# Two attention layers: the product with the values two steps behind the scores instead of one

## The chip, the cores and the metric

The kernel runs on one core of a Trainium2 chip, in one launch. The metric is the device time of that launch in microseconds, the median of the runs; lower is better.

## The reference, cut to what matters

Four layers on x of 4 sequences x 1024 tokens x 128 channels. Each layer normalises x, computes s (a mixer) and g (a network), and sets `x = x + s * silu(g)`. The mixers are a state-space layer, two causal softmax attentions with 16 heads of 8 channels, and a linear attention; the networks are a quantized one, one with low-rank parts, and two with experts. The change concerns the two softmax attentions alone:

```python
# layer 1
scores = jnp.einsum('bhqd,bhkd->bhqk', q, k) / math.sqrt(dh)
scores = scores + alibi_bias(H, L, scores.dtype)[None]      # causal, -inf above the diagonal
attn = jax.nn.softmax(scores, axis=-1)
out = jnp.einsum('bhqk,bhkd->bhqd', attn, v)
...
# layer 2: q and k turned by rope, then
scores = jnp.einsum('bhqd,bhkd->bhqk', q, k) * D ** (-0.5)
scores = jnp.where(causal[None, None], scores, -jnp.inf)
weights = jax.nn.softmax(scores, axis=-1)
out = jnp.einsum('bhqk,bhkd->bhqd', weights, v)
```

## The kernel before, in words

`attention_layer` is called once for layer 1 and once for layer 2. Its work is cut into 16 groups (`NGB`), each of 4 heads of one sequence. A group has two chunks of 512 queries (`ch`), and runs over 12 steps (`key_steps`): blocks of 128 keys (`j`), 4 for the first chunk, 8 for the second. Because of causality the steps differ in width: the queries that see the block are 512, 384, 256 and 128 in steps 0 to 3; 512 in steps 4 to 8; 384, 256 and 128 in steps 9 to 11.

A step has two `scores` events, one for each pair of heads: PE multiplies keys by queries into one of two PSUM buffers (`sring`, tile a_st, L1530), with a mask product on the diagonal (L1533); ACT takes the exponential into `prob`, which has three buffers, one per step (L1653). Then a `values` event: four products of 9 columns (8 channels and the row sum) with the probabilities, one per head, go into the accumulator `acc`, each head into 32 partitions of its own (L1548). Since scores lie with keys on partitions, the row maximum has to be known before: for every group, one group ahead, `max` events compute queries by keys (tile a_mx, L1497, mask L1500 or L1492), DVE reduces each (L1743); when a chunk is complete DVE does six small operations on the maxima (L1749 to L1754), PE transposes them (`turn_max`, L1506), DVE copies, and SP sends them through DRAM into three extra rows of the queries.

When the last step of a chunk is accumulated, ACT copies `acc` into `osb` (L1660); the next chunk's first `values` waits for that copy. A `turn_out` event transposes `osb` on PE (L1558), and DVE divides by the row sums (L1764, L1770).

The results of `max`, `turn_max`, `turn_out` and of the projections share one ring of three PSUM buffers (`qring`, tile a_mx) in the order of the program: an event waits until the event three places before it has been emptied, by DVE or for some kinds by ACT.

All engines walk through the same list `order`, each doing its part, and wait for each other by counting semaphores. The list is made by a loop over groups, steps and pairs: at each score index (24 per group) it puts the events of other work that are due (projections of the next sequence, in layer 2 the scatters by POOL), then as many `max` events as a table of due times says, then `scores`. `values` of step s-1 comes after the scores of step s; the last step's comes at the end of the group. The turned output of the second chunk is put before the scores of step 2 of the next group, that of the first chunk after step 6. The main waits on PE:

```python
                            if s >= 2:
                                pe.wait_ge(exped, s - 1)       # scores number s of the layer
...
                            pe.wait_ge(exped, 2 * (v + 1))     # values number v of the layer
...
                            if j == 0 and chunk:
                                pe.wait_ge(o_evac, chunk)
```

Of the kernel before, what the change touches and what calls it, by code (L numbers as in the profile page):

```python
# [98 lines left out]
def build_program(nc, a, out, ctx):  # L99
# [1032 lines left out]
    def attention_layer(layer, seqs, loads, x_slots=None):  # L1132
# [10 lines left out]
        NGB = NG * BATCH  # L1143
        QB4 = NT // 2
        MROWS = PARTS * GH * QB4
        NP_, NR = 3, 3
        STEPS = 24


# [20 lines left out]
        for G in range(1, NGB):  # L1170
            due[STEPS * G + 8 - LEAD] = unit_end[2 * G + 1]
        due[STEPS * NGB] = len(ahead)
        due_at, due_n = sorted(due), [due[k] for k in sorted(due)]
        key_steps = [(ch, j) for ch in range(2) for j in range(4 * ch + 4)]
# [55 lines left out]
        placed_at.sort(key=lambda v: v[0])  # L1230

        order, done, put = list(prelude), 0, 0
        late = None
        for G in range(NGB):
            for s, (ch, j) in enumerate(key_steps):
                for pair in range(2):
                    index = STEPS * G + 2 * s + pair
                    while put < len(placed_at) and placed_at[put][0] <= index:
                        order.append(placed_at[put][1])
                        put += 1  # L1240
                    goal = math.ceil(np.interp(index, due_at, due_n))
                    order += ahead[done:goal]
                    done = max(done, goal)
                    if (s, pair) == (2, 0) and G:
                        order.append(("turn_out", G - 1, 1))
                    order.append(("scores", G, ch, j, pair))
                if s:
                    order.append(("values", G, *key_steps[s - 1]))
                if s == 6:
                    order.append(("turn_out", G, 0))  # L1250
            order.append(("values", G, *key_steps[-1]))
        order.append(("turn_out", NGB - 1, 1))
        order += [e for _, e in placed_at[put:]] + back_events(BATCH - 1)

        at = {}
# [20 lines left out]
        with ExitStack() as c:  # L1276
# [30 lines left out]
            else:  # L1307
# [10 lines left out]
            ring_made, ring_v, ring_a, m_ready, st_made, exped, pv_done, o_evac, step, astep = (  # L1318
                sem(n + k) for k in ("ring_made", "ring_v", "ring_a", "m_ready", "st_made", "exped", "pv_done", "o_evac",
                                     "step", "astep"))  # L1320
# [1540 lines left out]
```

## Time and profile before

| | |
|---|---|
| median of 3 runs | 2873.87 us |
| lowest, highest | 2872.76, 2879.74 us |
| span of the profiled execution | 2867.6 us, 6.3 us under the median of the runs; its own time outside the profiler is not known |
| PE | 2232.3 us busy (78%) |
| DVE | 1650.8 us busy (58%) |
| ACT | 1246.7 us busy (43%) |
| POOL | 727.9 us busy (25%) |

All times in the views are microseconds from the start of the span. PE is the matmul engine and PEld its weight loads, which run ahead of the matmuls; DVE, ACT and POOL are the vector, scalar and GpSimd engines, SP the queue that issues most DMAs. In a timeline row stand the start, the duration, the engine, the line, what is written from what, shapes and types, and the number of instructions merged in the row; in brackets the idle time of the engine before it and what ended it. The ends of matmuls are modelled and overlap the next start, so that on PE the distance between two starts is the cost of the first. A `values` event shows as 8 matmuls.

### The profile page before, as it was taken

To read this page: it belongs to the slowest core of one execution; us is meant where nothing else is said; L and a number is where in the kernel's file an instruction comes from. 1 tells how busy PE (TensorE), PEld (TensorE's weight loads), DVE (VectorE), ACT (ScalarE), POOL (GpSimd) and SP (SyncE) were. 2 spreads that over 40 slices of the span, in tenths; PEclk is the share of its full clock that TensorE was granted. 3 is DMA by queue.
4 is the path that set the end of the run, shared out by engine and by line. 5 is a ranking of instruction groups with operands and counts; after the bars stand their busy time and mean duration, and the time that the engine had idled before them with its cause. 6 is when DMAs were issued, how large, how long until landed. Compare 5 with 4: busy or idle time off the path is not lost. (4 is left out here: it accounts for less than half of the span.)

```text
span 2867.6 us, 44223 instructions
## 1 busy us (share of the span) xinstructions
PE 2232.3 (78%) x15437; PEld 1302.5 (45%) x15454; DVE 1650.8 (58%) x3303; ACT 1246.7 (43%) x1901; POOL 727.9 (25%) x870
## 2 busy tenths in 40 slices
PE   3778878863899989999740389999999788777474
PEld 2555555542344444444340134444443686455274
DVE  6676767631677747567049277777775343553201
ACT  2343434320466656565520046565666343332143
POOL 1435353441010101000000223233322113663432
PEclk8898888876899999999755599999999899896597
DMA  2111100012011101110000302121210895110185
GB/s 62 39 53 53 46 2 2 2 44 85 2 55 40 54 24 32 46 36 20 1 1 3 106 22 77 42 79 40 79 54 27 257 321 185 41 41 22 38 274 182
DMA packets 144303, 185.77 MB, mean 65 GB/s; under 512 B 26970, under 2 KB 118267, under 8 KB 138976
## 3 DMA queue, kind: packets, MB, share of 16 engines
q1 hardware_dynamic: 103295, 137.52, 16.0%
q0 software_dynamic: 13696, 32.02, 3.5%
q10 hardware_dynamic: 27126, 13.75, 1.7%
q8 instruction: 117, 1.92, 0.3%
q14 instruction: 69, 0.57, 0.1%
HBM read 130.46 MB, written 52.21 MB: 64 GB/s over the span
## 5 line engine op out<-in xcount | busy, mean ns | idle before, releaser
L1743 DVE TENSOR_REDUCE a_mpart<-a_mx 128x1 f32<-128x512 f32 (+3 forms) x1216 | 741.2, 655 | 284.4 <-PE a_mx L1497 148.8
L1653 ACT ACTIVATE a_prob<-a_st 128x1024 f32<-128x1024 f32 (+3 forms) x768 | 607.1, 812 | 487.8 <-PE a_st L1533 374.4
L1497 PE MATMUL a_mx<-a_ka,a_qa 96*128 96x512 bf16 (+3 forms) x1536 | 428.8, 339 | 31.6 <-DVE a_mpart L1743 14.4
L1530 PE MATMUL a_st<-a_qa,a_ka 96*128 96x512 bf16 (+3 forms) x1536 | 416.3, 333 | 29.9 <-ACT a_prob L1653 22.8
L1548 PE MATMUL a_acc<-a_prob,a_v_aug 128*9 128x512 f32 (+3 forms) x3072 | 321.1, 494 | 0.0
L1497 PEld LDWEIGHTS a_mx<-a_ka,a_qa 96*128 96x128 bf16 x1536 | 140.7, 99 | 315.6 <-DVE a_mpart L1743 175.4
L1426 POOL DMA_INDIRECT x_rows<-l_xn,l_slots x128 | 125.4, 980 | 400.0 <-ACT a_prob L1653 390.0
L1533 PE MATMUL a_st<-w_mask_t,identb 128*128 128x128 bf16 x1024 | 208.8, 224 | 0.0
L1530 PEld LDWEIGHTS a_st<-a_qa,a_ka 96*128 96x128 bf16 x1536 | 145.7, 99 | 136.5 <-ACT a_prob L1653 38.6
L2084 PE MATMUL t_psu<-t_xsT,t_w 128*128 128x128 f32 x960 | 152.8, 294 | 23.9 <-DMA t_w<-in_l_experts 17.4
L1500 PE MATMUL a_mx<-w_mask_q,identb 128*128 128x128 bf16 x768 | 165.2, 225 | 0.0
L1968 POOL DMA_INDIRECT b_back<-y_rows,l_slots x128 | 134.1, 1048 | 71.8 <-issue 36.3
L2084 PEld LDWEIGHTS t_psu<-t_xsT,t_w 128*128 128x128 f32 x960 | 130.1, 203 | 36.6 <-issue 25.4
L1079 POOL TENSOR_TENSOR l_sqr<-l_yg 128x256 f32<-128x256 f32 x64 | 39.3, 614 | 280.2 <-DVE l_yg L932 277.6
L1533 PEld LDWEIGHTS a_st<-w_mask_t,identb 128*128 128x128 bf16 x1024 | 102.2, 100 | 15.5 <-issue 2.6
L2201 DVE TENSOR_TENSOR t_h<-t_sg,t_psu 128x128 f32<-128x128 f32 x160 | 45.9, 288 | 101.9 <-ACT t_sg L2149 98.6
L903 DVE TENSOR_TENSOR_SCAN l_lmat<-l_job,l_ident 128x1024 f32<-128x1024 f32 x32 | 73.1, 2288 | 45.2 <-PE l_job L564 44.7
L1548 PEld LDWEIGHTS a_acc<-a_prob,a_v_aug 128*9 128x9 f32 x3072 | 45.9, 88 | 109.8 <-issue 81.1
L1465 POOL TENSOR_TENSOR x<-x,a_prod 128x512 f32<-128x512 f32 x8 | 10.2, 1269 | 309.4 <-DVE a_prod L1831 309.4
L1764 DVE RECIPROCAL a_rden<-a_mx 128x16 f32<-128x16 f32 x64 | 16.1, 252 | 122.4 <-PE a_mx L1558 122.4
L1500 PEld LDWEIGHTS a_mx<-w_mask_q,identb 128*128 128x128 bf16 x768 | 77.1, 100 | 13.5 <-issue 8.3
L1436 POOL TENSOR_TENSOR l_xn<-x,a_st 128x512 f32<-128x512 f32 x8 | 8.1, 1040 | 281.9 <-DVE a_st L1777 281.9
(438 smaller groups left out, 4055.0 us busy)
## 6 DMA issues: line engine op xcount, KB each, us to landing
t_w<-in_l_experts SPq DMA_DIRECT2D x160, 192.0 KB, 4.2
t_w<-in_l_experts SPq DMA_DIRECT2D x40, 514.0 KB, 7.4
a_qa<-q_parts_dram SPq DMA_DIRECT2D x96, 192.0 KB
a_ka<-k_parts_dram SPq DMA_DIRECT2D x96, 192.0 KB
x_rows<-zeros SPq DMA_DIRECT2D x25, 512.0 KB, 3.6
t_xs<-x_rows ACTq DMA_DIRECT2D x40, 256.0 KB, 4.9
y_rows<-t_y POOLq DMA_DIRECT2D x40, 256.0 KB, 5.1
q_parts_dram<-a_parts SPq DMA_DIRECT2D x24, 256.0 KB, 3.0
```

What stands on the lines that cost most here:

```text
L903: dve.tensor_tensor_scan(to, flat(e), ident8[:].rearrange("p t i -> p (t i)"), 0.0, ALU.mult, ALU.add).then_inc(ring_v, 1)
L1426: pool.indirect_dma_start(x2_rows, bass.IndirectOffsetOnAxis(x_slots[:, k, b * NT + t:b * NT + t + 1], 0), seqs[b].xn[:, t], None, bounds_ ...
L1497: ins = pe.matmul(to, qa[G % NQ][:, h0 + k, qi * P:(qi + 1) * P], ka[G % NQ][:, h0 + k, lo:hi], start=not masked_first, stop=k == per - 1 ...
L1500: ins = pe.matmul(to[:, width - P:width], identb[:], diagonal, start=False, stop=True)
L1530: ins = pe.matmul(to[:, lo:HALF], ka[G % NQ][:, h, j * P:(j + 1) * P], qa[G % NQ][:, h, ch * HALF + lo:(ch + 1) * HALF], start=True, stop= ...
L1533: ins = pe.matmul(to[:, lo:lo + P], identb[:], W["mask_t"][:], start=False, stop=True)
L1548: ins = pe.matmul(acc[h * SLOT:h * SLOT + DH + 1, lo:HALF], v_aug[:, b % 2, j, G % NG * GH + h], prob[:, v % NP_, h, lo:HALF], start=j == ...
L1653: act.activation(prob[:, v % NP_, 2 * pair:2 * pair + 2, lo:HALF], sring[s % 2][:, :, lo:HALF], ACT.Exp, scale=1.0 if alibi else scale).th ...
L1743: dve.tensor_reduce(mpart[:, G % 2, h0:h0 + per, qi, piece], slot[:, 0:per * width].rearrange("p (k w) -> p k w", k=per), X, ALU.max).then ...
L1968: pool.indirect_dma_start(dst, None, rows, bass.IndirectOffsetOnAxis(slots[:, t:t + 1], 0), bounds_check=rows.shape[0] - 1).then_inc(arriv ...
L2084: ins = pe.matmul(psu[k % 4][:, m * P:(m + 1) * P], w[:, k, m * P:(m + 1) * P], rhs, start=True, stop=True)
L2201: dve.tensor_tensor(h[:, k % 4], sg[:, k % 4], psu[k % 4][:, P:2 * P], ALU.mult).then_inc(h_ready, 1)
```

## The change

The loop now keeps a list `steps` of all `values` events of the layer, and puts the one that lies two steps back (`BACK = 2`) after each step's scores, across the ends of groups too; only the last two of the layer stand together, at its end. The turned output of the second chunk moves from before step 2 to before step 4 of the next group, that of the first chunk from after step 6 to after step 7. Nothing else changes: the same instructions, buffers and waits.

```diff
         NP_, NR = 3, 3
+        BACK = 2
         STEPS = 24
...
         order, done, put = list(prelude), 0, 0
-        late = None
+        steps = [("values", G, *step) for G in range(NGB) for step in key_steps]
...
-                    if (s, pair) == (2, 0) and G:
+                    if (s, pair) == (4, 0) and G:
                         order.append(("turn_out", G - 1, 1))
                     order.append(("scores", G, ch, j, pair))
-                if s:
-                    order.append(("values", G, *key_steps[s - 1]))
-                if s == 6:
+                current = len(key_steps) * G + s
+                if current >= BACK:
+                    order.append(steps[current - BACK])
+                if s == 7:
                     order.append(("turn_out", G, 0))
-            order.append(("values", G, *key_steps[-1]))
-        order.append(("turn_out", NGB - 1, 1))
+        order += steps[len(steps) - BACK:] + [("turn_out", NGB - 1, 1)]
```

All lines behind the first edit have numbers higher by one in the changed kernel.

Two places show what moves. The first is on PE, in layer 2, at the end of one group (number 6 of 0 to 15). Before, from the last scores of the group (keys and queries in buffers ka0, qa0) to the first of the next (ka1, qa1); the maxima (mx) are of the group after:

```order
4983 L1530 MATMUL a2_st1<-a2_qa0,a2_ka0 128x128
4984 L1533 MATMUL a2_st1<-w_mask_t,identb 128x128
4985 L1548 MATMUL a2_acc<-a2_prob,a2_v_aug 9x256 x4
4986 L1548 MATMUL a2_acc<-a2_prob,a2_v_aug 9x128 x4
4987 L1497 MATMUL a2_mx0<-a2_ka2,a2_qa2 128x384
4988 L1500 MATMUL a2_mx0<-w_mask_q,identb 128x128
4989 L1497 MATMUL a2_mx1<-a2_ka2,a2_qa2 128x384
4990 L1500 MATMUL a2_mx1<-w_mask_q,identb 128x128
4991 L1530 MATMUL a2_st0<-a2_qa1,a2_ka1 128x512
```

The changed kernel at the same scores, and its next block behind the two scores of the new group's step 0:

```order
4982 L1531 MATMUL a2_st1<-a2_qa0,a2_ka0 128x128
4983 L1534 MATMUL a2_st1<-w_mask_t,identb 128x128
4984 L1549 MATMUL a2_acc<-a2_prob,a2_v_aug 9x384 x4
4985 L1498 MATMUL a2_mx0<-a2_ka2,a2_qa2 128x384
...
4997 L1531 MATMUL a2_st1<-a2_qa1,a2_ka1 128x512
4998 L1534 MATMUL a2_st1<-w_mask_t,identb 128x128
4999 L1549 MATMUL a2_acc<-a2_prob,a2_v_aug 9x256 x4
5000 L1498 MATMUL a2_mx0<-a2_ka2,a2_qa2 128x512
```

The blocks of steps 10 (9x256) and 11 (9x128) stood together; now step 9's (9x384) ends the group, and step 10's follows the new group's first scores.

The second place is on PE, some rows further, at steps 1 and 2 of the new group. Before:

```order
5014 L1530 MATMUL a2_st1<-a2_qa1,a2_ka1 128x384
5015 L1533 MATMUL a2_st1<-w_mask_t,identb 128x128
5016 L1548 MATMUL a2_acc<-a2_prob,a2_v_aug 9x512 x4
5017 L1497 MATMUL a2_mx1<-a2_ka2,a2_qa2 128x512
5018 L1558 MATMUL a2_mx2<-ident,a2_osb 128x128 x4
...
5023 L1497 MATMUL a2_mx0<-a2_ka2,a2_qa2 128x512
5024 L1506 MATMUL a2_mx1<-identb,a2_mparts 48x128
```

The changed kernel there, and down to its turned output before step 4:

```order
5015 L1549 MATMUL a2_acc<-a2_prob,a2_v_aug 9x128 x4
5016 L1498 MATMUL a2_mx1<-a2_ka2,a2_qa2 128x512
...
5021 L1498 MATMUL a2_mx2<-a2_ka2,a2_qa2 128x512
5022 L1507 MATMUL a2_mx0<-identb,a2_mparts 48x128
...
5040 L1549 MATMUL a2_acc<-a2_prob,a2_v_aug 9x384 x4
5041 L1498 MATMUL a2_mx1<-a2_ka2,a2_qa2 128x512
5042 L1498 MATMUL a2_mx2<-a2_ka2,a2_qa2 128x512
5043 L1559 MATMUL a2_mx0<-ident,a2_osb 128x128 x4
```

Between the last score of step 1 and the transposed maxima (48x128) a block of 128 columns stands where one of 512 stood, and the turned output (from osb) is gone from there.

## Rows read from the trace of the kernel before

**Rows 1.** Windows: layer 1, layer 2, a group, the last group; per engine busy (x).
```profile
750.60:1432.00 681.40, 628.35 (x4658) 297.03 (x4656) 430.63 (x907) 411.34 (x536) 47.63 (x42) 0.95 0.11 33
1652.40:2222.30 569.90, 549.53 (x4283) 243.42 (x4284) 423.30 (x887) 339.59 (x458) 167.02 (x163) 0.99 0.18 53
1919.58:1952.29 32.71, 32.03 (x263) 14.00 (x262) 26.11 (x57) 19.87 (x27) 5.84 (x6) 1.00 0.18 52
2197.66:2222.30 24.64, 22.15 (x192) 7.81 (x185) 1.10 (x4) 19.62 (x27) 4.86 (x5) 1.00 0.05 15
```

**Rows 2.** Waits in layer 2: who waited for whom, us, times, longest.
```profile
PEld a_mx L1497 <- DVE a_mpart L1743: 91.9, 161, 1.3
```

**Rows 3.** The accumulator's tile, whole span: what its instructions waited for, us, times.
```profile
  ACT a_prob L1653: 22.2, 60
  PE a_acc L1548: 17.7, 32
```

**Rows 4.** Timeline of PE's weight loads at a group's end.
```profile
1918.24 0.12 PEld L1548 LDWEIGHTS a_acc<-a_prob,a_v_aug 128*9 128x9 f32 x8
1918.78 0.12 PEld L1548 LDWEIGHTS a_acc<-a_prob,a_v_aug 128*9 128x9 f32 x8 [0.42 <-ACT a_prob L1653]
1919.12 0.10 PEld L1497 LDWEIGHTS a_mx<-a_ka,a_qa 96*128 96x128 bf16 x1 [0.22 <-issue]
```

**Rows 5.** Timeline of PE: blocks of the values with their neighbours.
```profile
1895.97 0.62 PE L1548 MATMUL a_acc<-a_prob,a_v_aug 128*9 128x256 f32 x8
1896.52 0.39 PE L1497 MATMUL a_mx<-a_ka,a_qa 96*128 96x512 bf16 x1
...
1922.99 1.05 PE L1548 MATMUL a_acc<-a_prob,a_v_aug 128*9 128x512 f32 x8
1923.97 0.39 PE L1497 MATMUL a_mx<-a_ka,a_qa 96*128 96x512 bf16 x1
...
1926.14 0.22 PE L1533 MATMUL a_st<-w_mask_t,identb 128*128 128x128 bf16 x1
1926.20 0.27 PE L1530 MATMUL a_st<-a_qa,a_ka 96*128 96x256 bf16 x1
...
1926.32 0.22 PE L1533 MATMUL a_st<-w_mask_t,identb 128*128 128x128 bf16 x1
1926.46 0.83 PE L1548 MATMUL a_acc<-a_prob,a_v_aug 128*9 128x384 f32 x8
1927.23 0.39 PE L1497 MATMUL a_mx<-a_ka,a_qa 96*128 96x512 bf16 x1
```

**Rows 6.** Timeline of PE at steps 1 and 2 of a group.
```profile
1924.20 0.60 PE L1558 MATMUL a_mx<-ident,a_osb 128*128 128x128 f32 x4
1924.64 0.27 PE L1530 MATMUL a_st<-a_qa,a_ka 96*128 96x256 bf16 x1
...
1925.26 0.39 PE L1497 MATMUL a_mx<-a_ka,a_qa 96*128 96x512 bf16 x1
1925.86 0.24 PE L1506 MATMUL a_mx<-identb,a_mparts 128*48 128x128 bf16 x1 [0.20 <-DVE a_mpart L1743]
```

**Rows 7.** Timeline of DVE, the same stretch.
```profile
1919.56 3.77 DVE L1743 TENSOR_REDUCE a_mpart<-a_mx 128x1 f32<-128x384 f32 x6 [0.87 <-PE a_mx L1500]
...
1924.52 1.28 DVE L1743 TENSOR_REDUCE a_mpart<-a_mx 128x1 f32<-128x512 f32 x2
```

**Rows 8.** Timeline of PE behind the first chunk's turned output.
```profile
1904.23 0.66 PE L1558 MATMUL a_mx<-ident,a_osb 128*128 128x128 f32 x4
1904.72 0.33 PE L1497 MATMUL a_mx<-a_ka,a_qa 96*128 96x384 bf16 x1
...
1905.76 0.22 PE L1500 MATMUL a_mx<-w_mask_q,identb 128*128 128x128 bf16 x1
1906.03 0.39 PE L1497 MATMUL a_mx<-a_ka,a_qa 96*128 96x512 bf16 x1
```

**Rows 9.** Timeline of ACT: the accumulator's copies at the last group's start and end.
```profile
2197.91 0.59 ACT L1660 COPY a_osb<-a_acc 128x512 f32<-128x512 f32 x1 [0.53 <-PE a_acc L1548]
2221.57 0.59 ACT L1660 COPY a_osb<-a_acc 128x512 f32<-128x512 f32 x1 [0.53 <-PE a_acc L1548]
```

**Rows 10.** Timeline of PE at step 11 of a group.
```profile
1917.68 0.34 PE L1497 MATMUL a_mx<-a_ka,a_qa 96*128 96x384 bf16 x1 [0.20 <-DVE a_mpart L1743]
```

## The prediction

> **What bounds the kernel now.** First the busy time by stretch [rows 1]: the two attention layers take 681.4 and 569.9 us, nearly half of the span of 2867.6 us, and the change touches nothing else. In the second, PE is busy 549.5 of 569.9 us, DVE 423.3 and ACT 339.6: PE sets the pace. A group (four heads of one sequence) that carries no projections takes 32.71 us, and PE is busy for 32.03 of them. So what counts is what PE's own queue loses. Next the waits [rows 2]: PE's weight loads for the row maxima wait for DVE 161 times, 91.9 us in all; a load may wait early while PE still multiplies, so this is a bound, and the true loss must be read from PE's timeline. Last the values tile [rows 3]: its loads waited for the exponential 22.2 us in 60 cases, and ACT waited 17.7 us in 32 cases (one per group) for the last product of a group before it could copy the accumulator out. These two waits are what the change aims at.
>
> **Are they real?** Inside a group no values product waits for anything. Scores number n wait until exponential n-2 is done; scores (s, pair 1) thus wait for the last exponential of step s-1, and the product of step s-1 follows behind. Its wait is met when PE gets there, at a distance of one as of two. The exception is the group's end, where the products of steps 10 and 11 stand in a row. There [rows 4] the product of step 10 begins at 1918.24, that of step 11 at 1918.78, the next maximum at 1919.12. Step 10's product has 256 columns, and one that stands alone takes 1896.52 - 1895.97 = 0.55 us [rows 5]: as long as the 0.54 here. The load's wait of 0.42 us lies wholly under it. The change can win nothing on PE at the group's end.
>
> **Costs of the blocks.** A product of 512 columns takes 0.98 us, one of 384 0.77 (1926.46 to 1927.23) [rows 5], 256 0.55, 128 0.34 (1918.78 to 1919.12) [rows 4]. Before each block PE loses some time: 1926.32 to 1926.46 is 0.14 us for a mask product of 128 columns that otherwise takes 0.06 (1926.14 to 1926.20) [rows 5]. So 0.08 to 0.09 go at each entry, and blocks with it cost 1.07, 0.86, 0.64 and 0.43. A pair in a row pays one entry; the change splits it in 30 of 32 groups (the last of each layer stays a pair): 30 x 0.08 = 2.4 us. Does leaving the block cost too? The Trainium skill, TensorEngine Tiling (Array Packing), section Tiling Modes, says that changing the tiling mode drains TensorE; the products use 32 columns of the array each, their neighbours all of it. If that held on the way out as well, the 0.12 us by which 0.98 exceeds 4 x 512 columns at 2.4 GHz would belong to the switch, and the term would be 6 us. The trace speaks against it: in the pair, step 10's product shows the same 0.54 with no switch behind it. I take 2.4.
>
> **The moved work against DVE's ring.** Maxima, the transposed maxima and the turned outputs share three buffers that DVE empties, so PE waits where it issues them faster than DVE works. I follow the group from 1919.12, writing the shift of the changed kernel against the trace.
> (1) Before the last two maxima of the group stands step 9's block (0.86) instead of the pair (0.98): -0.12.
> (2) DVE reduces six blocks from 1919.56 to 1923.33, and its next reduction starts at 1924.52 [rows 7], since six small operations for the chunk's maxima lie between (1.19 us). Step 10's block (0.64) now stands in the midst of the six: DVE, fed about 0.4 us late, starts these small operations 0.47 later. PE waits here in both kernels. Before, the maximum at 1925.26 and the transposed maxima at 1925.86 wait for DVE's reductions [rows 6]: PE could have been there 0.29 and then 0.37 us sooner, 0.66 together. Now the turned output is gone from between, and the transposed maxima need the buffer one reduction (0.6) earlier: 1925.86 + 0.47 - 0.6 = 1925.73, shift -0.13. But by then PE has done less: the 1.07 block and the turned output (0.44, 1924.20 to 1924.64) are still to come, for 0.64 + 0.43. The wait has grown from 0.66 to about 1.1.
> (3) In step 2 follows 1.07 instead of 0.86: +0.08.
> (4) Steps 3 to 5 have blocks 0.86, 0.64, 0.43 instead of 0.64, 0.43, 1.07: -0.21; the turned output is paid here, +0.44, and the second maximum behind it waits for a buffer, about +0.22 (DVE needs some 1.8 us, with start and two reductions of 0.6 to 0.7, for what PE issues in 1.6). Shift +0.53.
> (5) The other turned output goes from step 6 to step 7. Behind it PE waited: 1905.76 to 1906.03 is 0.27 for 0.06, plus 0.05 in the 0.49 us from 1904.23 [rows 8]. In step 7 it stands after full blocks with DVE idle: -0.25. Shift +0.28.
> (6) In step 10 the block is 1.07 instead of 0.86. PE waits for DVE behind it (0.20 shown as idle before the maximum at 1917.68 [rows 10], some 0.7 in all three waits there), which swallows the 0.21.
> So such a group loses about 0.28 us, the extra entry of 0.08 included. Groups with projections have PE work of another kind between: there the wait in (4) goes, and the waits of (2) are partly DVE's for the projections. Followed the same way: +0.14 for one of the four kinds, +0.3 and +0.06 for the others. Mean 0.2, times 30 is 6 us; ends 0 and 0.5 (no wait added in (2) and (4), or both everywhere), 0 to 15 us.
>
> **The last group and the first.** The last has no maxima beside it; 24.64 us [rows 1], ACT and PE take turns. ACT's first copy waits 0.53 us there [rows 9], which the change removes, but the blocks move one step towards the end, where exponentials are short and PE sets the pace: one more 1.07 block behind the full ones, less what ACT and PE catch up. I get the last copy (2221.57 [rows 9]) 0.7 us later, 1.4 for two layers; ends -1 and +2.1. The first groups lack one block before they are under way: -0.6, ends 0 and -1.
>
> Other queues: SP's loads and POOL's scatters wait for exponentials counted by scores, whose order stays. The third buffer of exponentials is free before it is needed, since product s-3 stands in PE's queue before scores s. Cost nothing; if PE ran late there, scores would be late too.
>
> **Sum**: 6 + 1.4 - 0.6 = 6.8 us on 2867.6, a span of 2874.4. The median shown is 6.3 us above that span, so 2880.7.
>
> **Rivals.** (A) ACT's wait and copy at the group's end do count: 0.53 + 0.59 us for 30 groups would be 34 us, 2840. Against it: ACT is busy 60% of the time. A weaker form is likelier: the spread turned outputs save the waits of (2) and (5), 0.66 + 0.25, and nothing takes their place; less the 0.08 that is 0.83 x 30 = 25 us, 2849. For it: a 0.5 us DVE job leaves the tightest spot. Against it: six small operations stay, and PE's cover goes as well. Together 9%.
> (B) The wait behind the transposed maxima: it grows from 0.66 to 1.1 in all groups and the one of (4) comes everywhere, so 0.5 us per group, 15 us, 2889. It decides once a group loses over 0.29 us on average, since 0.3% (about what a measurement of this kernel can tell from no change) is 8.6 us. My own sum is near that point. 38%.
> (C) The distance is of no consequence at all: waits just change places. Then 2.4 us, 2876; it shares the verdict of my forecast. Forecast and (C) 53%.
>
> **Numbers.** Likeliest 2880.7, within 0.3%. Range 2864 to 2892: above it (B) with 1 us more per layer, below a gain of 10 us. Faster 9%, same 53%, slower 38%.
>
> **What would show it.** ACT's wait for the accumulator gone from all but the last groups: right by construction. The pair split, with blocks of 0.55 and 0.34 us and an entry before each. The group at 1919.58, 32.71 us long, at 33.0. PE's idle time before the transposed maxima up by some 0.4 us a group, behind the turned output of step 6 gone. If that group comes out at 32.3 or less, step (2) is wrong and a rival of gain holds; at 33.3 or more, (B).

## The result, and the profile after

| | before | changed |
|---|---|---|
| median of 20 runs each | 2876.51 us | 2886.48 us |
| lowest, highest | 2861.44, 2892.02 us | 2876.79, 2896.15 us |
| ratio | | 1.0039, 95% interval 1.0024 to 1.0053 |
| span of the profiled execution | 2867.6 us | 2884.2 us (its own time 2886.17) |

The change makes the kernel slower by 0.39%, some 10 us. The forecast was no measurable change, with 6.8 us lost. The measured time lies inside the range, but by the bound of 0.3% it is the slower case that came true; the interval still holds that bound. The profiled execution of before was a short one: its span lies 8.9 us below the median of the 20 runs, where a kernel's own time exceeds its span by 2.0 us (2886.17 against 2884.2). So the difference of the two spans, 16.6 us, is more than the change costs by about the 6.9 us by which that execution was short.

The windows of the changed kernel that answer to [rows 1], layer 1, layer 2, the group without projections and the last group (window, length, then busy us and count of PE, PEld, DVE, ACT and POOL, granted clock, share of the DMA engines, GB/s):

```profile
754.10:1443.00 688.90, 631.64 (x4654) 298.10 (x4653) 430.65 (x905) 408.63 (x536) 47.47 (x42) 0.94 0.12 32
1663.20:2241.00 577.80, 552.68 (x4283) 246.03 (x4283) 421.20 (x887) 336.02 (x458) 166.96 (x163) 0.98 0.18 52
1935.41:1968.44 33.03, 31.77 (x263) 14.05 (x262) 26.02 (x57) 19.65 (x26) 5.83 (x6) 1.00 0.19 51
2216.10:2241.00 24.90, 23.10 (x204) 8.15 (x200) 1.10 (x4) 19.04 (x27) 4.85 (x5) 1.00 0.05 15
```

The group went from 32.71 to 33.03 us, as forecast (33.0), and PE is busy 0.26 us less in it: what was added is waiting. ACT, DVE and POOL do the same work as before. But both layers grew by more than the groups explain, and the granted clock fell by 0.01 in each. The windows of [rows 1] and these do not end at the same event. Taken from the first scores to the start of the accumulator's last copy (before at 2221.57, [rows 9], changed in the row below), the last group of layer 2 went from 23.8 us (2197.78 to 2221.57) to 24.6 (2216.10 to 2240.68), layer 1 grew by 8.8 us (679.0 to 687.8) and layer 2 by 8.3 (569.2 to 577.5).

```profile
2240.68 0.58 ACT L1661 COPY a_osb<-a_acc 128x512 f32<-128x512 f32 x1 [1.02 <-PE a_acc L1549]
```

The tile of the accumulator (what its instructions waited for, us, times), beside [rows 3]:

```profile
  ACT a_prob L1654: 15.8, 43
  PE a_acc L1549: 3.0, 2
```

ACT waited for the accumulator 32 times and now does twice, at the end of each layer. What the change aims at has happened. The first row still has 43 cases at a distance of two steps: a weight load goes early and waits while PE still multiplies, so most of this row never was PE's time.

PE's timeline of the group without projections, from its first values block down to step 4, beside [rows 6]:

```profile
1936.89 0.62 PE L1549 MATMUL a_acc<-a_prob,a_v_aug 128*9 128x256 f32 x8
1937.44 0.39 PE L1498 MATMUL a_mx<-a_ka,a_qa 96*128 96x512 bf16 x1
...
1939.48 0.41 PE L1549 MATMUL a_acc<-a_prob,a_v_aug 128*9 128x128 f32 x8
1939.82 0.39 PE L1498 MATMUL a_mx<-a_ka,a_qa 96*128 96x512 bf16 x1
...
1940.38 0.38 PE L1498 MATMUL a_mx<-a_ka,a_qa 96*128 96x512 bf16 x1
1941.74 0.24 PE L1507 MATMUL a_mx<-identb,a_mparts 128*48 128x128 bf16 x1 [0.98 <-DVE a_mpart L1744]
...
1942.35 1.04 PE L1549 MATMUL a_acc<-a_prob,a_v_aug 128*9 128x512 f32 x8
1943.33 0.39 PE L1498 MATMUL a_mx<-a_ka,a_qa 96*128 96x512 bf16 x1
...
1945.98 0.60 PE L1559 MATMUL a_mx<-ident,a_osb 128*128 128x128 f32 x4
```

The pair is split, into blocks of 0.55 (1936.89 to 1937.44) and 0.34 us (1939.48 to 1939.82). A maximum of 512 columns takes 0.23 us from its start to the next start (1937.44 to 1937.67 on this timeline); the one at 1940.38 is followed by the transposed maxima only at 1941.74. So PE waits 1.36 - 0.23 = 1.13 us here, where before it waited 0.66 in two pieces. The 1.07 us block now stands behind the wait and not before it. The same place on DVE's timeline:

```profile
1937.92 1.89 DVE L1744 TENSOR_REDUCE a_mpart<-a_mx 128x1 f32<-128x512 f32 x3 [0.79 <-PE a_mx L1501]
...
1940.91 0.17 DVE L1755 TENSOR_TENSOR a_mparts<-a_mneg,a_mparts 128x16 bf16<-128x16 f32 x1
1941.01 1.88 DVE L1744 TENSOR_REDUCE a_mpart<-a_mx 128x1 f32<-128x512 f32 x3
```

DVE ends the last of its six small operations at 1941.08, goes on with a reduction, and when that has freed its buffer (0.6 us after 1941.01), PE's transposed maxima may start. From 1937.92 on it does not idle until the maxima are out: the ring of three buffers bounds PE here, as step (2) had it. Before that it stood idle for 0.79 us, since PE had step 10's block to do first; the six reductions that stood together in [rows 7] are now three and three, and the small operations start later.

Then the part that no step of the forecast spoke of. Windows of 2 us in group 1 of layer 2, same columns:

```profile
1722.00:1724.00 2.00, 0.68 (x6) 0.31 (x4) 1.81 (x7) 1.79 (x4) 0.72 (x1) 1.00 0.00 0
1724.00:1726.00 2.00, 1.75 (x13) 0.50 (x13) 1.51 (x4) 0.60 (x1) 1.88 (x2) 0.66 0.11 37
1726.00:1728.00 2.00, 2.00 (x14) 0.62 (x7) 0.52 (x1) 0.00 (x0) 0.28 (x1) 0.50 0.04 6
1728.00:1730.00 2.00, 2.00 (x22) 1.00 (x21) 1.46 (x3) 1.27 (x3) 0.31 (x1) 0.99 0.38 51
```

PE was busy for only 0.68 us of the first window. This kind of group (1, 5 and 9 of the layer) has 20 us of POOL's work beside it, and here the wait before the transposed maxima is the longest of the groups 1 to 14. Shortly afterwards the granted clock is at 0.50, the level of 1.2 GHz, and back at 2.4 GHz just after 1728. PE's timeline there and at the same place of group 5:

```profile
1724.25 0.24 PE L1507 MATMUL a_mx<-identb,a_mparts 128*48 128x128 bf16 x1 [1.57 <-DVE a_mpart L1744]
...
1725.00 1.90 PE L1549 MATMUL a_acc<-a_prob,a_v_aug 128*9 128x512 f32 x8
1726.83 0.61 PE L1498 MATMUL a_mx<-a_ka,a_qa 96*128 96x512 bf16 x1
...
1871.74 0.24 PE L1507 MATMUL a_mx<-identb,a_mparts 128*48 128x128 bf16 x1 [1.57 <-DVE a_mpart L1744]
...
1872.35 1.04 PE L1549 MATMUL a_acc<-a_prob,a_v_aug 128*9 128x512 f32 x8
1873.33 0.39 PE L1498 MATMUL a_mx<-a_ka,a_qa 96*128 96x512 bf16 x1
```

The same wait of 1.57 us stands before both. In group 1 the block behind it takes 1.83 us (1725.00 to 1726.83), in group 5 0.98. The three such groups of the layer, 1, 5 and 9:

```profile
1715.56:1753.98 38.42, 36.64 (x270) 15.81 (x269) 29.40 (x61) 23.14 (x33) 19.96 (x19) 0.96 0.18 48
1863.05:1899.90 36.85, 35.08 (x271) 15.54 (x270) 29.31 (x61) 23.14 (x33) 19.96 (x19) 1.00 0.17 49
2008.96:2047.39 38.43, 36.65 (x271) 15.95 (x270) 29.41 (x61) 23.14 (x33) 19.95 (x19) 0.96 0.17 47
```

At full clock this group is even 0.2 us shorter than before, where all three took 37.05 to 37.07 at a clock of 1.00, with a longest single wait of 1.09 us at this place of group 1. A fall costs 1.57 us (38.42 - 36.85).

**Where the 10 us went.** Both kernels were profiled a second time (next section). From the first scores of each group to those of the next (for the last group to the start of the last copy), means of two profiles each, the two layers grew by 7.6 and 7.3 us. In layer 2: 2.1 in the first group, 0.8 in the last, 3.1 in two falls of the clock per execution, and 1.3 in the other difference of groups 1 to 14, that is 0.1 a group. In layer 1: 0.7 in the first group, 2.1 in the last, 0.9 in the ten groups 1 to 5, 8, 9 and 12 to 14, and 3.9 in the groups 6, 7, 10 and 11. In the two profiles of before each of these four groups repeats within 0.02 us; changed, they differ by 1.6, 3.1, 0.1 and 3.9 us between one profile and the next. The sum of 14.9 is above the 10 us by which the medians differ; two profiles each do not fix it better.

### The profile page after: what moved, and what is told of

It is laid out like the page before. It is cut to its first block and busy times, and to the rows that moved or that the text cites. A ratio compares the mean times of both kernels' runs of the same rounds, so it can differ in the third digit from the quotient of the medians.

```text
span 2884.2 us, 44240 instructions
## 1 busy us (share of the span) xinstructions
PE 2246.5 (78%) x15454; PEld 1308.2 (45%) x15454; DVE 1648.4 (57%) x3303; ACT 1240.0 (43%) x1901; POOL 727.0 (25%) x870
## 5 line engine op out<-in xcount | busy, mean ns | idle before, releaser
L1549 PE MATMUL a_acc<-a_prob,a_v_aug 128*9 128x512 f32 (+3 forms) x3072 | 328.7, 502 | 0.1
L2085 PE MATMUL t_psu<-t_xsT,t_w 128*128 128x128 f32 x960 | 151.4, 292 | 23.4 <-DMA t_w<-in_l_experts 14.9
L1969 POOL DMA_INDIRECT b_back<-y_rows,l_slots x128 | 133.9, 1046 | 71.7 <-issue 36.3
```

The costliest lines, as they stand in the source:

```text
L1549: ins = pe.matmul(acc[h * SLOT:h * SLOT + DH + 1, lo:HALF], v_aug[:, b % 2, j, G % NG * GH + h], prob[:, v % NP_, h, lo:HALF], start=j == ...
L1969: pool.indirect_dma_start(dst, None, rows, bass.IndirectOffsetOnAxis(slots[:, t:t + 1], 0), bounds_check=rows.shape[0] - 1).then_inc(arriv ...
L2085: ins = pe.matmul(psu[k % 4][:, m * P:(m + 1) * P], w[:, k, m * P:(m + 1) * P], rhs, start=True, stop=True)
```

## The experiments

Each was timed beside runs of the kernel before on the same chip; medians of before were 2874.11 us for the first four, 2873.76 for the next four, 2878.46 for the last three. Unless the text names another kernel, a diff is against the kernel before, and "the group" is the one without projections in layer 2, which took 32.71 us before and 33.03 changed. Its length repeats within 0.02 us in the two profiles of either kernel, so it tells apart what the total, whose single runs spread over 20 to 30 us, cannot.

### The distance alone

The changed kernel with its turned outputs at the old places (the diff is against the changed kernel):

```diff
-                    if (s, pair) == (4, 0) and G:
+                    if (s, pair) == (2, 0) and G:
...
-                if s == 7:
+                if s == 6:
```

> The values two steps behind, the turned outputs where the kernel before had them (before step 2, after step 6). Ring theory (what costs is PE waiting behind the transposed maxima, because a 1.07 us block is gone from step 1): the turned output before step 2 must now wait for ACT's copy of the accumulator, which comes late, and takes a buffer; the projection-free group of layer 2 (32.70 us before, 33.02 in the change) takes about 33.2. Rival, the moved turned outputs are what costs: it goes back to 32.7 to 32.8. Time: ring theory 6 us above the change at most, rival 8 us below it.

Measured: 2891.0 us, ratio 1.0054 (1.0033 to 1.0074); the group 33.24 us. Its window, and the turned output before step 2 on PE's timeline:

```profile
1934.98:1968.22 33.24, 32.05 (x263) 13.92 (x262) 26.11 (x57) 19.86 (x26) 5.83 (x6) 1.00 0.18 51
```
```profile
1940.58 0.63 PE L1559 MATMUL a_mx<-ident,a_osb 128*128 128x128 f32 x4 [0.81 <-ACT a_osb L1661]
```

The distance by itself costs 0.53 us a group. Part of it is a wait that the change does not have: at its old place the turned output must now wait for ACT's copy. Groups 1, 5 and 9 took 37.22 to 37.23 us at a clock of 1.00. PE's wait in them is in pieces (0.81 us before the turned output, 0.35 to 0.36 and 0.20 behind it), and no fall of the clock followed.

### The turned outputs alone

```diff
-                    if (s, pair) == (2, 0) and G:
+                    if (s, pair) == (4, 0) and G:
...
-                if s == 6:
+                if s == 7:
```

> The turned outputs moved as in the change, the values one step behind as before. Ring theory: the 1.07 us block stays before the transposed maxima, which need a buffer one reduction earlier (-0.59), the turned output is paid in step 3 with a wait of 0.22 behind it (+0.66), the wait after step 6 goes (-0.25): the projection-free group takes 32.5 us, the kernel some 5 us less than before. Rival, the moved turned outputs are what costs: 33.0 us per group, some 9 us more.

Measured: 2864.06 us, ratio 0.9967 (0.9952 to 0.9981); the group 32.48 us. Its window, and PE's timeline before the transposed maxima:

```profile
1913.89:1946.37 32.48, 31.74 (x262) 14.03 (x261) 26.01 (x57) 19.74 (x27) 5.83 (x6) 1.00 0.18 52
```
```profile
1918.85 0.38 PE L1497 MATMUL a_mx<-a_ka,a_qa 96*128 96x512 bf16 x1
1919.57 0.24 PE L1506 MATMUL a_mx<-identb,a_mparts 128*48 128x128 bf16 x1 [0.34 <-DVE a_mpart L1743]
```

This half of the change wins 0.23 us a group and 0.33% in all. The wait before the transposed maxima is 0.72 - 0.23 = 0.49 us, less than the 0.66 of before. So the change is a gain and a larger loss: -0.23 and +0.53 give +0.30, and the group shows +0.32. That they add up so well should not be pressed, since the wait for ACT's copy stands in the one kernel alone. The weaker form of rival (A) named this gain, at 0.83 us a group; it is 0.23, and in the change the distance takes it back.

### The split of the pair alone

```diff
+                    if (s, pair) == (0, 0) and G:
+                        order.append(("values", G - 1, *key_steps[-1]))
                     order.append(("scores", G, ch, j, pair))
...
-            order.append(("values", G, *key_steps[-1]))
-        order.append(("turn_out", NGB - 1, 1))
+        order += [("values", NGB - 1, *key_steps[-1]), ("turn_out", NGB - 1, 1)]
```

> The kernel before with one edit: the last block of a group (step 11) stands behind the next two maxima instead of directly behind step 10's. It prices the split pair alone. Rows of before: 0.08 to 0.10 us per group for one more entry, 32.8 us per projection-free group, 3 us for the kernel. Rival, both changes of tiling drain TensorE (0.2 us): 32.9 us, 6 us.

Measured: 2877.55 us, ratio 1.0025 (1.0004 to 1.0046); the group 32.81 us. The split costs 0.10 us a group, close to the 0.08 that the forecast charged for one more entry. That this number was right for a wrong reason came out with the next two kernels.

### The distance, but the last three blocks together at the group's end

Against the changed kernel:

```diff
-                if current >= BACK:
+                if s >= BACK:
                     order.append(steps[current - BACK])
...
-        order += steps[len(steps) - BACK:] + [("turn_out", NGB - 1, 1)]
+            order += steps[current + 1 - BACK:current + 1]
+        order.append(("turn_out", NGB - 1, 1))
```

> The change, but a group's last three blocks stand together at its end, so steps 0 and 1 of the next have none. It has one entry less than before. Ring theory: nothing covers DVE's small operations in steps 0 and 1, PE waits about 1.6 us before the transposed maxima (0.66 before, 1.1 in the change): the projection-free group takes 33.3 us although it has fewer entries, the kernel 15 us or more above before. Rival, the split pair is what costs: 32.6 us, the time of before.

Measured: 2886.21 us, ratio 1.0055 (1.0039 to 1.0071); the group 33.03 us, not 33.3. The wait before the transposed maxima came out at the 1.6 us that was expected. So 0.3 us had been saved elsewhere. Its window, and PE's weight loads at the group's end:

```profile
1930.41:1963.44 33.03, 31.32 (x263) 14.41 (x262) 26.02 (x57) 19.64 (x27) 5.83 (x6) 1.00 0.18 51
```
```profile
1961.56 0.12 PEld L1550 LDWEIGHTS a_acc<-a_prob,a_v_aug 128*9 128x9 f32 x8
1961.90 0.11 PEld L1550 LDWEIGHTS a_acc<-a_prob,a_v_aug 128*9 128x9 f32 x4 [0.21 <-issue]
1962.22 0.54 PEld L1550 LDWEIGHTS a_acc<-a_prob,a_v_aug 128*9 128x9 f32 x12 [0.21 <-issue]
1962.98 0.10 PEld L1499 LDWEIGHTS a_mx<-a_ka,a_qa 96*128 96x128 bf16 x1 [0.22 <-issue]
```

From 1961.56 to 1962.98 the blocks of 384, 256 and 128 columns take 1.42 us. Alone they take 0.77 + 0.55 + 0.34 = 1.66. Two of three had another values block behind them, and 0.24 us are gone: 0.12 for each exit that did not take place. By columns, 4 x 768 at 2.4 GHz are 1.28 us, plus one exit 1.40.

### The pair behind the next group's first two maxima

```diff
+                    if (s, pair) == (0, 0) and G:
+                        order += [("values", G - 1, *step) for step in key_steps[-2:]]
                     order.append(("scores", G, ch, j, pair))
-                if s:
+                if 0 < s < len(key_steps) - 1:
                     order.append(("values", G, *key_steps[s - 1]))
...
-            order.append(("values", G, *key_steps[-1]))
-        order.append(("turn_out", NGB - 1, 1))
+        order += [("values", NGB - 1, *step) for step in key_steps[-2:]] + [("turn_out", NGB - 1, 1)]
```

> The kernel before, with the last two blocks of a group together behind the next two maxima. The run with three blocks in a row showed 1.42 us for 384, 256 and 128 columns, not 0.77 + 0.55 + 0.34 = 1.66: a block costs 0.12 less when another follows that need not wait. New theory: leaving a block costs 0.11 to 0.12 us (the array drains), and in the kernel before step 11's block hid that in a real wait of 0.11 for the exponential. Then the pair takes 0.77 us here instead of 0.88 and the projection-free group of layer 2 32.6 us instead of 32.70. Rival, as the prediction read it (step 10's block takes its own 0.54 and nothing waits): the pair stays at 0.88, the group at 32.7.

Measured: 2876.97 us, ratio 1.0007 (0.9987 to 1.0026), no difference in the total; the group 32.60 us, as expected if the exit costs. The window, and the pair's weight loads with the first of the next score:

```profile
1933.86:1966.46 32.60, 31.90 (x264) 14.06 (x260) 26.02 (x57) 19.86 (x26) 5.82 (x6) 1.00 0.18 52
```
```profile
1965.69 0.55 PEld L1549 LDWEIGHTS a_acc<-a_prob,a_v_aug 128*9 128x9 f32 x16 [0.21 <-issue]
1966.46 0.10 PEld L1531 LDWEIGHTS a_st<-a_qa,a_ka 96*128 96x128 bf16 x1 [0.22 <-issue]
```

The same two blocks take 0.77 us here (1965.69 to 1966.46) and took 0.88 in [rows 4] (1918.24 to 1919.12). The exponential is ready here: there is no wait for ACT in the row. (What follows the pair differs too, scores in place of a maximum.) So in the kernel before PE did lose 0.11 us at the group's end. By columns the pair is 4 x 384 at 2.4 GHz, 0.64 us, and one exit makes 0.76.

### The second turned output later still

As the turned outputs alone, but `(s, pair) == (5, 0)` in place of `(4, 0)`.

> The turned outputs alone moved, the second chunk's to before step 5 instead of step 4. Ring theory: the wait of 0.22 us behind it goes, since the full blocks of steps 4 and on give DVE time: group 32.26 against 32.48 with step 4, the kernel 6 us less than that one. Rival, DVE's total work sets the wait and it turns up elsewhere: 32.48.

Measured: 2865.4 us, ratio 0.9971 (0.9957 to 0.9985); the group 32.34 us, 0.14 less than with step 4. With the turned output before step 4 PE waited for a buffer behind it, which step (4) of the forecast priced at 0.22. In that kernel two maxima take 0.58 us there (1924.25 to 1924.83) and 0.44 elsewhere (1922.94 to 1923.38), so the wait was 0.14, and moving the turned output wins all of it.

### Values blocks in pairs throughout

Against the changed kernel:

```diff
-                    if (s, pair) == (4, 0) and G:
+                    if (s, pair) == (5, 0) and G:
...
-                if current >= BACK:
-                    order.append(steps[current - BACK])
+                if current >= BACK and s % 2 == 0:
+                    order += steps[current - BACK:current]
```

> Values in pairs everywhere: after the scores of each even step the blocks of the two steps before, six pairs per group instead of ten blocks and a pair; turned outputs before step 5 and after step 7. Drain theory: five entries (0.09) and five exits (0.12) fewer, and no wait for the exponential: -1.16 us per group; the turned outputs give -0.4; but steps 0 to 2 have no full block before the transposed maxima, which costs up to 0.9: 32.0 to 32.4 us. Rival, only entries cost: -0.45 - 0.4 + 0.9, 32.75 us.

Measured: 2892.81 us, ratio 1.0070 (1.0046 to 1.0095), and yet the group takes 32.27 us, 0.76 less than in the changed kernel: six entries and six exits are saved in each group. It is the slowest kernel of all with one of the shortest groups. The last group takes 26.03 us, and groups 1, 5 and 9 of layer 2 take 37.8, 37.6 and 36.3, the first two with falls of the clock. But the loss is in layer 1: from the first scores to the last copy layer 2 takes 568.4 us, no more than in the two profiles of before (569.2 and 571.5), and layer 1 takes 695.1 against 679.0 and 675.0. Its first group takes 55.4 us (52.2 before), groups 7 and 11 take 56.5 and 57.1 (52.4 and 52.5), its last 59.2 (57.0 and 52.9). Why pairs cost so much there was not isolated; that two blocks together leave a longer stretch without cover before the next is the likeliest reason, not a shown one.

### Pairs only where they cover something

The blocks stand alone before the transposed maxima, in pairs elsewhere, and the last pair behind the next two maxima; `turn_out` as in the kernel with step 5.

```diff
+        VALUES_AFTER = {1: (0,), 3: (1, 2), 4: (3,), 6: (4, 5), 8: (6, 7), 10: (8, 9)}
...
-                    if (s, pair) == (2, 0) and G:
+                    if (s, pair) == (5, 0) and G:
                         order.append(("turn_out", G - 1, 1))
+                    if (s, pair) == (0, 0) and G:
+                        order += [("values", G - 1, *step) for step in key_steps[-2:]]
                     order.append(("scores", G, ch, j, pair))
-                if s:
-                    order.append(("values", G, *key_steps[s - 1]))
-                if s == 6:
+                order += [("values", G, *key_steps[k]) for k in VALUES_AFTER.get(s, ())]
+                if s == 7:
                     order.append(("turn_out", G, 0))
-            order.append(("values", G, *key_steps[-1]))
-        order.append(("turn_out", NGB - 1, 1))
+        order += [("values", NGB - 1, *step) for step in key_steps[-2:]] + [("turn_out", NGB - 1, 1)]
```

> Blocks in the order 0 after step 1 (it covers the transposed maxima as before), 1 and 2 after step 3, 3 after step 4, 4 and 5 after step 6, 6 and 7 after 8, 8 and 9 after 10, 10 and 11 behind the next two maxima; turned outputs before step 5 and after step 7. Drain and ring theory together: four entries and exits fewer (-0.84), no wait for the exponential (-0.11), turned outputs -0.44: 31.3 us per projection-free group, up to 31.8 if DVE's ring waits longer behind pairs; the kernel 25 to 40 us less than before. Rival, exits cost nothing: 31.8 to 32.2 us, 15 to 25 us less.

Measured: 2863.03 us, ratio 0.9963 (0.9948 to 0.9979); the group 31.43 us, but the total gained some 11 us and not 25 or more. Its window, and a pair of two blocks of 512 columns on PE's timeline:

```profile
1915.90:1947.33 31.43, 30.88 (x265) 14.68 (x261) 25.68 (x57) 19.73 (x26) 5.82 (x6) 1.00 0.18 54
```
```profile
1931.54 1.90 PE L1549 MATMUL a_acc<-a_prob,a_v_aug 128*9 128x512 f32 x16
1933.38 0.34 PE L1498 MATMUL a_mx<-a_ka,a_qa 96*128 96x384 bf16 x1
```

The pair takes 1.84 us, two single blocks 2 x 0.98: once more 0.12 for the missing exit. Of the 1.28 us that the group won, 0.37 are the turned outputs (32.34 in the kernel with step 5), so fewer switches and the wait for the exponential are worth 0.91; four entries and four exits at 0.09 and 0.12, with 0.11 for the wait, are 0.95. The total did not gain as much: the last group of layer 2 took 25.87 us against 23.8 (it has no maxima to stand beside ACT's work), group 9 of layer 2 37.5 us at a clock of 0.95, where group 1 took 35.99 at 1.00, and in layer 1 groups 6, 7, 10 and 11 together took 212.5 us against 203.3, as much more as its ten other groups from 1 to 14 won.

### The chosen version

Against the last one: one by one where pairs leave PE idle, in the last group of each layer and in layer 1 in two of each four groups from the fifth on.

```diff
-                order += [("values", G, *key_steps[k]) for k in VALUES_AFTER.get(s, ())]
+                one_by_one = G == NGB - 1 or alibi and G >= NG and G % NG >= 2
+                after = ((s - 1,) if 0 < s < 11 else ()) if one_by_one else VALUES_AFTER.get(s, ())
+                order += [("values", G, *key_steps[k]) for k in after]
```

> Paired blocks only where DVE sets the waits; one by one in the last group of each layer and in layer 1's groups with the second network (every third and fourth from the fifth on), where ACT takes turns with PE. The last two blocks behind two maxima and the turned outputs at step 5 and after step 7 everywhere. Drain and ring theory: the projection-free group of layer 2 at 31.4 us, the last group of layer 2 back from 25.9 to 23.3 us, the kernel 18 to 25 us less than before. Rival, what pairs win is lost to ACT in any arrangement: no better than the 2863 to 2865 us of the two best so far.

Measured: 2859.4 us (6 runs), ratio 0.9936 (0.9919 to 0.9953): 0.64% faster than before and, by the two ratios, 1.0% faster than the changed kernel. Against the last kernel nothing is settled: its interval and this one overlap. The last group:

```profile
2188.20:2211.50 23.30, 21.96 (x188) 7.82 (x184) 1.10 (x4) 19.04 (x26) 4.85 (x5) 1.00 0.05 16
```

23.30 us to the start of the last copy, against 23.8 before and 24.6 changed. The group is 31.43 us as in the last kernel, and groups 6, 7, 10 and 11 of layer 1 take 201.2 us together instead of 212.5. Falls of the clock in groups 1 and 5 of layer 2 remain (37.96 and 38.20 us at a clock of 0.96, where group 9 takes 36.44 at 1.00).

### Both kernels once more

The changed kernel, and the one before, unedited.

> The change once more, for the groups of layer 2 that carry projections of q and k (1, 5 and 9). In the first profile two of them took 38.4 us and one 36.85; the two had a granted clock of 0.5 for 3.4 us right after PE's wait of 1.57 us before the transposed maxima. Clock theory: the same wait stands in all three, and any of them may fall; each takes 36.85 at full clock and 38.4 with the fall. Rival, a DMA or GpSimd hold-up in groups 1 and 9: these two take 38.4 again, with the clock at 1.00.

> The kernel before once more. Clock theory: its waits before the transposed maxima are shorter (1.08 and 0.20 us in group 5), so groups 1, 5 and 9 of layer 2 stay at 37.05 to 37.07 us with no clock under 1.00; what differs from the first profile lies in groups of layer 1 with long waits for ACT. Rival: any group may fall, also these three.

Measured: 2887.1 and 2872.44 us. The changed kernel's groups 1, 5 and 9 of layer 2:

```profile
1713.64:1752.12 38.48, 36.70 (x271) 16.05 (x270) 29.50 (x61) 23.14 (x33) 19.97 (x19) 0.96 0.17 48
1861.22:1899.55 38.33, 36.55 (x270) 15.74 (x269) 29.33 (x61) 23.14 (x33) 19.96 (x19) 0.96 0.16 47
2008.64:2045.51 36.87, 35.09 (x271) 15.55 (x270) 29.34 (x61) 23.14 (x33) 19.98 (x19) 1.00 0.17 49
```

Again two of three have a fall, this time 1 and 5 and not 1 and 9, while the kernel before again had none (37.08, 37.07, 37.07 us). So falls in these groups come with the changed order, and which of the three they hit differs from one execution to the next. The rival of a hold-up by a DMA or GpSimd at full clock is out: the long groups show a clock of 0.96. All other groups of the changed kernel's layer 2 but the first repeat within 0.02 us; of the kernel before, group 4 differs by 0.2 us and groups 6 and 10 by under 0.1. The two profiles of before differ otherwise in the last group of layer 1 and the first of layer 2, and not in the groups of layer 1 with long waits, as had been expected.

## Why the prediction was right or wrong

**Direction, mechanism and the group: right.** The wait of ACT went and was worth nothing. The wait before the transposed maxima grew from 0.66 to 1.13 us (forecast 1.1), because the long block that covered it stands behind it now; the group came out at 33.03 us (forecast 33.0), the last group of layer 2 at +0.8 (forecast +0.7). Behind the first chunk's turned output PE no longer waits. Step (2) was about 0.06 us too low: from the group's start to the transposed maxima 6.33 us (1941.74 - 1935.41), against 6.28 (1925.86 - 1919.58) and a forecast of 6.27. Step (4) was 0.08 too high, its wait being 0.14. Step (5) counted 0.05 us of the 0.49 for the turned output as a wait; in the changed kernel it takes 0.50 (1956.24 to 1956.74), again right behind a values block, so this stayed, and 0.21 was won and not 0.25. The three errors nearly cancel.

**The mean over the groups: 0.2 forecast, 0.1 measured.** The group without projections was forecast right (+0.28, measured +0.32). The three other kinds of layer 2, forecast between +0.06 and +0.3, measured +0.2, +0.2 and, at full clock, -0.2. The term of 6 us for 30 groups is more like 3, with the falls of the clock and the groups 6, 7, 10 and 11 of layer 1 left out.

**"The trace speaks against it ... I take 2.4": wrong.** This was the sentence on the exit. It rested on the pair showing "the same 0.54 with no switch behind it", and on the claim that the wait of 0.42 us for the exponential "lies wholly under it". Each had covered up the other. Step 10's block has no exit and takes 0.43 us; the missing 0.11 was a true wait of PE for the exponential. The pair with its exponential ready takes 0.77 us, the three blocks together 1.42 and not 1.66, two of 512 columns 1.84 and not 1.96. The Trainium skill, TensorEngine Tiling (Array Packing), section Tiling Modes, says that changing the mode drains TensorE, without a word on the direction; the runs agree with it, at 0.11 to 0.12 us on the way out beside 0.08 to 0.09 on the way in. That the blocks are fp32 between bf16 products is not what costs: the four fp32 transposes of [rows 6], which use the whole array, start at 1924.20, 1924.31, 1924.42 and 1924.53, and the scores behind them at 1924.64, so the last is as short as the others, and the maximum ahead of them takes 0.23 us like any other. The term itself hardly suffered: the split costs an entry and an exit, 0.09 + 0.12, and does away with the wait of 0.11, which makes 0.10, just what the split alone measured. But the wrong reading hid the best use of the place. A whole family of orders with fewer switches was worth 0.9 us a group, and "the change can win nothing on PE at the group's end" was true only because the switch ate the gain.

**No step spoke of the clock: the term that was missing.** The forecast priced a wait at its own length. In the changed kernel waits of 1.57 us in groups 1, 5 and 9 of layer 2 were followed in two of three cases by the level of 1.2 GHz, each fall at a further 1.6 us: 3.1 us an execution, more than twice the 1.3 us that groups 1 to 14 of the layer lose otherwise. It is one of the parts that carried the total past the forecast, and not the largest: by the means of two profiles each, groups 6, 7, 10 and 11 of layer 1 lost 3.9 us, the first groups 2.8 where -0.6 was forecast, the last groups 2.9 where 1.4 was. That the total still came out within the range is in part luck: the groups that the forecast worked out gave half of its 6 us, and parts that it had not, or had with the other sign, made it up.

**The first groups: wrong.** Forecast -0.3 each, measured +0.7 in layer 1 and +2.1 in layer 2. The first group of layer 2, before and changed:

```profile
1652.40:1701.80 49.40, 45.51 (x308) 18.91 (x309) 40.31 (x85) 20.62 (x27) 11.23 (x11) 0.93 0.04 13
```
```profile
1663.20:1715.60 52.40, 48.01 (x293) 19.65 (x294) 40.64 (x85) 20.32 (x26) 11.14 (x11) 0.87 0.04 12
```

The clock is 0.93 before and 0.87 changed, and PE is busy 2.5 us more for the same products, which is what a slower clock looks like. In the repeats it was 0.89 and 51.25 us before, and 52.42 us changed. Before, one of its transposed maxima starts over 1.4 us after the instruction ahead of it (1.86 us), changed there are two (1.57 and 1.86). The changed trace shows PE idle for 1.35 us before 1675.69 and 1.47 before 1685.84, and the clock at 0.50 from 1676.86 to 1680.27 and from 1687.10 to 1690.51, soon after each; its repeat shows the same two falls. In the profiles of before the one wait of 1.48 us was followed by no fall (49.4 us) and by one (51.25 us). So the length of this group goes with the number of falls. But no run isolated the new wait, nor the 3.9 us of the groups 6, 7, 10 and 11 in layer 1: of group 11 the windows show the same, before and changed:

```profile
1208.70:1261.20 52.50, 46.93 (x336) 23.98 (x335) 26.27 (x55) 33.82 (x41) 0.00 (x0) 0.94 0.09 25
```
```profile
1215.90:1271.40 55.50, 49.89 (x336) 24.41 (x335) 26.24 (x56) 33.91 (x41) 0.00 (x0) 0.88 0.08 24
```

In the group of 55.5 us the clock stands at 0.50 for 13.7 us, in the one of 52.5 for 6.8 us. That the clock goes with these groups' time is shown; what in the new order lowers it there is left open, and so is the last group of layer 1 (+2.1, forecast +0.7), which differed by 4.1 us between the two profiles of before.

**The rivals.** (A) fell as a forecast for the change, but the half of it that the turned outputs make is real (-0.33%). (B) gave the right verdict by a wrong road: it expected 0.5 us in every group, and the groups lose 0.1; its point of decision, 0.29 us a group on average, was passed only with what the falls of the clock, the long groups of layer 1 and the first and last groups added. (C) is refuted by the first two kernels: distance and turned outputs each move the time, in opposite directions.

**The median.** The forecast added 6.3 us to the span, the distance to the median of 3 runs. Only 2.0 of that lies around the span; the rest was that the profiled execution had been shorter than the median. Over 20 runs the median of before is 2876.51 us and not 2873.9, so of the 5.8 us by which 2880.7 was too low, 2.6 lie in the time of before and 3.2 in the change, which costs 10 us where 6.8 were forecast.

## What to carry to other kernels

Price a block that is moved by what it covered at its old place: the wait it uncovers there counts in full, and a wait removed from another engine counts nothing while that engine has slack. When two readings of one duration are possible (a wait or a switch that happen to be equally long), a run that makes the data ready tells them apart, and no argument does. Where small blocks need another tiling, put them side by side, except where a single block is the cover in front of a slower engine's chain, and keep the waits that remain short, since one long wait may cost the clock as well.

## What the runs showed of the hardware

- A values block costs about 0.2 us beside its columns: 0.08 to 0.09 where PE goes over to the blocks' tiling, 0.11 to 0.12 where it leaves it, at 2.4 GHz.
- The four heads of a block do not run one after the other. In the block of 256 columns at 1928.67 of the kernel before, the eight matmuls start in two sets of four, 0.007 us apart within a set and 0.22 from set to set. So the 4 in "4 x 256 columns" is what this form takes per column here, and not the number of heads.
- A wait of 1.57 us in an otherwise full stream of PE was followed by 1.2 GHz in four of the six cases in two profiles of the changed kernel, and by nothing in the other two; waits of 1.08 to 1.09 us at the same place of the kernel before, and one of 1.36 us before its transposed maxima at 2196.14, by nothing. So the length of the wait alone does not decide it. A fall was worth 1.5 to 1.6 us. The traces of all 13 profiles say the same for groups 1 to 14 of layer 2: of 132 groups whose longest idle time of PE was under 1.2 us none had a fall, of 37 with 1.2 to 1.5 us three had, of 13 with more seven. The longest, 2.24 us in the run with the last three blocks together, stands three times and was followed by a fall once.
- A small DVE operation can be held up while POOL works. In the kernel before, group 5 of layer 2:

```profile
1852.83 1.28 POOL L1448 TENSOR_TENSOR a_f<-a_f,a_turned 128x512 f32<-128x512 f32 x1
...
1853.26 0.89 DVE L1750 TENSOR_SCALAR a_mneg<-a_mneg 128x16 f32<-128x16 f32 x1
```

It began inside POOL's product and ended with it (1854.15 and 1854.11). Of the 64 operations of this line 57 take 0.17 us and seven take 0.28 to 0.90; all seven overlap a POOL instruction and end with it. Of the five other small operations only one case, a cast of 0.42 us, was held up, of 46 that overlap POOL. In the changed kernel the operation takes 0.52 to 0.53 us in groups 1, 5 and 9 of layer 2, 0.35 more than elsewhere. That stands in the chain before the transposed maxima, and is part of why PE's wait there is 1.57 us and not the 0.98 of the group without projections.
